# Attention block on one core: the last head pair's work spread evenly, 8 sums on TensorE, products on GpSimd, x loaded in 12 pieces

## What is computed

```python
xn = group_norm(x, 32 groups) * gn_w + gn_b
q, k, v = split(qkv_w @ xn + qkv_b)         # 8 heads of 64 channels
w = softmax(q^T k / sqrt(64))               # over the keys
a = v w^T                                   # 512 x T
out = xn + proj_w @ a + proj_b
```

## Time and profile before

| | before |
|---|---|
| median of 3 runs | 3740.59 us |
| lowest, highest | 3740.57, 3741.36 us |
| profiled execution, time | 3741.51 us |
| its span, first to last instruction | 3739.7 us |
| granted TensorE clock, mean | 0.998 |
| PE, PEld busy | 99%, 61% |
| DVE, ACT, POOL busy | 60%, 77%, 80% |
| instructions | 74752 |

### The profile page before, as it was taken

The page is one execution under the profiler, slowest core; times in us unless marked ns, Lnnn a source line. Parts: engine busy times, 40 slices in busy tenths (PEclk is TensorE's granted clock), DMA queues, the critical chain, the costliest instruction groups (busy, mean ns, idle before and its releaser), DMA issues.

```text
span 3739.7 us, 74752 instructions
## 1 busy us (share of the span) xinstructions
PE 3700.3 (99%) x30072; PEld 2267.9 (61%) x30072; DVE 2261.2 (60%) x2885; ACT 2875.0 (77%) x4091; POOL 2997.6 (80%) x1639
## 2 busy tenths in 40 slices
PE   8999999999999999999999999999999999999998
PEld 5565565656756565565675656556577565656556
DVE  6555657656565656665656565666655665565654
ACT  3777777787677777779767777777876777777885
POOL 1888888888388888888838888888875888888994
PEclk9999999999999999999999999999999999999999
DMA  2000012021400001201140000211222000000022
GB/s 81 21 17 26 23 32 73 17 61 37 148 19 23 17 23 39 67 23 55 52 133 25 18 23 17 60 50 28 68 65 101 23 23 19 23 17 20 20 88 89
DMA packets 131418, 165.03 MB, mean 44 GB/s; under 512 B 61696, under 2 KB 107776, under 8 KB 130176
## 3 DMA queue, kind: packets, MB, share of 16 engines
q1 hardware_dynamic: 131072, 160.26, 13.6%
HBM read 122.17 MB, written 38.04 MB: 43 GB/s over the span
## 4 chain that ended last, share of the span: by engine, by line
PE 93%; ACT 2%; POOL 2%; DVE 1%; issue 1%; DMA 0%; SPq 0%; ACTq 0%; POOLq 0%; DVEq 0%
PE oacc L648 29%; PE scores L627 23%; PE pool_bank L575 14%; PE aux_banks L597 12%; PE pool_bank L587 7%; PE scores L725 5%; POOL denom L1221 2%; PE pool_bank L614 1%; ACT probs L834 1%; ACT scores L847 1%; PE scores L575 1%; DVE maxima L953 1%; DVE stats L984 0%; PE scores L587 0%; DMA xn<-x 0%
## 5 line engine op out<-in xcount | busy, mean ns | idle before, releaser
L1221 POOL TENSOR_TENSOR denom<-denom,probs 128x768 f32<-128x768 f32 x1536 | 2821.9, 1837 | 422.0 <-ACT probs L834 230.6
L953 DVE TENSOR_REDUCE maxima<-aux_banks 128x2 f32<-128x512 f32 x1728 | 1655.9, 958 | 1305.8 <-PE aux_banks L597 1272.9
L834 ACT ACTIVATE probs<-scores 128x768 f32<-128x768 f32 x1728 | 1311.9, 812 | 679.7 <-PE scores L627 671.5
L847 ACT ACTIVATE scores<-seeds 128x768 f32<-128x768 f32 x1728 | 1342.6, 823 | 2.2 <-PE scores L635 1.5
L648 PE MATMUL oacc<-probs,vals 128*64 128x384 f32 x6912 | 1282.7, 492 | 0.0
L648 PEld LDWEIGHTS oacc<-probs,vals 128*64 128x64 f32 x6912 | 455.0, 136 | 522.7 <-issue 381.4
L597 PE MATMUL aux_banks<-k_hi,q_hi 64*128 64x512 f32 (+1 forms) x3456 | 681.3, 390 | 7.0 <-DVE maxima L953 6.4
L597 PEld LDWEIGHTS aux_banks<-k_hi,q_hi 64*128 64x128 f32 x3456 | 322.0, 183 | 534.8 <-issue 435.2
L627 PE MATMUL scores<-q_hi,k_hi 64*128 64x384 f32 x3456 | 597.4, 342 | 11.5 <-ACT scores L847 11.2
L627 PE MATMUL scores<-q_hi,k_lo 64*128 64x384 f32 x3456 | 586.5, 335 | 0.0
L627 PE MATMUL scores<-q_lo,k_hi 64*128 64x384 f32 x3456 | 586.0, 334 | 0.0
(11 more groups left out here) (93 smaller groups left out, 1534.0 us busy)
## 6 DMA issues: line engine op xcount, KB each, us to landing
seeds<-neg_rows SPq DMA_DIRECT2D x96, 384.0 KB, 3.5
xtile<-x SPq DMA_DIRECT2D x72, 384.0 KB, 3.2
att<-o_norm SPq DMA_DIRECT2D x96, 192.0 KB, 1.9
probs<-x SPq DMA_DIRECT2D x18, 768.0 KB, 4.5
out<-probs SPq DMA_DIRECT2D x18, 768.0 KB, 3.8
xtile<-att SPq DMA_DIRECT2D x12, 768.0 KB, 5.9
att_raw<-att SPq DMA_DIRECT2D x12, 768.0 KB, 6.8
xn<-x SPq DMA_DIRECT2D x7, 1152.0 KB, 12.7
```

The costliest lines, as they stand in the source:

```text
L834: a(prob(s).rearrange("p (h n) -> p h n", n=N), scores[:, s % 2, :, 0:N], ACT.Exp, scale=SCALE).then_inc(probs_ready, 1)
L847: a(scores[:, s % 2, :, 0:N], seeds[blk % 2][:, :].rearrange("p (e n) -> p e n", n=N), ACT.Copy).then_inc(seeded, 1)
L953: v.tensor_reduce(maxima[:, :, qt, kc], aux_banks[:, :, 0:UNIT_KEYS[kc % 2]], AX.X, ALU.max)\
L1221: gp.tensor_tensor(acc, acc, prob(s), ALU.add).then_inc(added, 1)
```

## The change

The last pair of a batch with a successor is planned by `SPREAD` like the inner ones, in the order own q, four k, one v, two k, two q, five v. The next batch's tiles are normalized from step 2, every 4 steps; each part waits for the own q chunks of its columns. `FINAL_OWN_Q` puts the quarters of the last batch's q chunks into the first 16 slots. The statistics of pair 2 stand at steps 30 to 52. The fourth piece (the product) is taken by GpSimd after the sum of the step before the put, for all blocks but the last of each batch and the last six of the last batch; the put is two steps later. In the last batch 8 of the last steps (3 in block 22, 5 in block 23, counted from 0) are not added by GpSimd: TensorE multiplies them with ones into the bank of the finish. In the last batch the odd chunks of `att` use `k_hi[0]` and `k_lo[0]`, and chunk 1 is split within the stream. x of the first batch comes in 12 transfers, and the weights are issued after the sixth has landed.

```diff
-    LAST_OWN_Q = ...
-    FINAL_OWN_Q = (((0, 0, 2), (1, 2, 4)), ((4, 0, 1), (6, 1, 2), (8, 2, 3), (10, 3, 4)),
-                   ((12, 0, 1), (14, 1, 2), (16, 2, 3), (18, 3, 4)), ((21, 0, 1), (23, 1, 2), (25, 2, 3), (27, 3, 4)))
-    LAST_RUNS = ((13, (1, 1, 2)), (16, (1, 1, 1, 1)),
-                 *((r + d, n) for r in (21, 30, 39) for d, n in ((0, (1, 1, 2)), (3, (1, 1, 2)), (6, (2, 2)))),
-                 *((r, (2, 2)) for r in (48, 50, 52)))
-    STATS_AT, STATS_EVERY = 28, 2
+    FINAL_OWN_Q = (((0, 0, 2), (1, 2, 4)), ((3, 0, 1), (4, 1, 2), (5, 2, 3), (6, 3, 4)),
+                   ((7, 0, 1), (8, 1, 2), (9, 2, 3), (10, 3, 4)), ((12, 0, 1), (13, 1, 2), (14, 2, 3), (15, 3, 4)))
+    STATS_AT, STATS_EVERY = 30, 2
-    NORM_AT, NORM_EVERY = 18, 2
+    NORM_AT, NORM_EVERY = 2, 4
...
+            if kind == LAST and more_batches:
+                items = own_q + next_k[0:4] + next_v[0:1] + next_k[4:] + next_q + next_v[1:]
+            elif kind == LAST:
+                items = []
+                for key, parts in zip(own_q, FINAL_OWN_Q):
+                    for s, a, b in parts:
+                        part(s0 + s, key, a, b)
+            else:
+                items = own_q + next_k + next_q + next_v
+            for n, key in enumerate(items):
+                for s, a, b in SPREAD[n % 3]:
+                    part(s0 + n // 3 * BLOCK_SLOTS + s, key, a, b)
...
-        att_hi = [att_hi0[:, :, :], four(k_hi[last_keys])]
-        att_lo = [att_lo0[:, :, :], four(k_lo[last_keys])]
+        def att_parts(tc, last):
+            keys = 1 - last_keys if last else last_keys
+            return (four(k_hi[keys]), four(k_lo[keys])) if tc % 2 else (att_hi0[:, :, :], att_lo0[:, :, :])
...
+        def summed_by_products(blk, kt, last):
+            return last and ((blk == BLOCKS - 2 and kt in (13, 15, 17)) or
+                             (blk == BLOCKS - 1 and kt in (9, 11, 13, 15, 17)))
+        def by_gpsimd(blk, last):
+            return blk < BLOCKS - (CH if last else 1)
         def put_at():
-            return {p * STEPS + fin_steps(j)[-1]: p * CH + j for p in range(PAIRS) for j in range(CH)
+            return {p * STEPS + fin_steps(j)[-1] + 2: p * CH + j for p in range(PAIRS) for j in range(CH)
...
-            for part in range(XPARTS):
+            for n in range(XITEMS):
+                i, part = n // XPARTS, n % XPARTS
                 cols_of = slice(part * XW, (part + 1) * XW)
-                sp.dma_start(xn[:, 0, cols_of], x[0, 0:128, cols_of]).then_inc(x00_in[part], 16)
-            for i in range(1, CT):
-                sp.dma_start(xn[:, i, :], x[0, i * 128:(i + 1) * 128, :]).then_inc(x0_in[i - 1], 16)
+                sp.dma_start(xn[:, i, cols_of], x[0, i * 128:(i + 1) * 128, cols_of]).then_inc(x0_in[n], 16)
+            sp.wait_ge(x0_in[XITEMS // 2 - 1], 16)
...
+            def sum_by_product(s, u, opens):
+                to = bank_for(u) if opens else bank(u)
+                for e in range(2):
+                    mm(to[head(e), 0:N], ones[:, :], prob(s)[:, e * N:(e + 1) * N], start=opens, stop=False)
...
+                if summed_by_products(s // KT, kt, last):
+                    sum_by_product(s, use(b, last, ("finish", p, t // KT)),
+                                   not any(summed_by_products(s // KT, k, last) for k in range(kt)))
...
-                            if NORM_STEPS[s] == 0:
-                                wait_full(act, use(b, last, ("q", PAIRS - 1, CH - 1)))
+                            if NORM_STEPS[s] and NORM_STEPS[s] % CT == 0:
+                                wait_full(act, use(b, last, ("q", PAIRS - 1, 2 * (NORM_STEPS[s] // CT) + 1)))
...
-                    if 0 <= n < CT:
-                        att_high(b, 0, slice(n, n + 1))
+                    if 0 <= n < (2 if last else 1) * CT:
+                        att_high(b, n // CT, last, slice(n % CT, n % CT + 1))
...
+                            if piece == PIECES - 1 and by_gpsimd(blk, last):
+                                continue
                             take_recip(b, blk, use(b, last, ("finish", blk // CH, blk % CH)), piece)
...
+                if summed_by_products(blk, kt, last):
+                    pool.wait_ge(added, PRIMED + ADDS * (BLOCKS * b + blk) + kt - 1)
+                    pool.sem_inc(added, 1)
+                    return
...
+            def normalize_block(n):
+                pool.wait_ge(recip_ready, PRIMED + n + 1)
+                pool.wait_ge(o_saved, PRIMED + n + 1)
+                pool.wait_ge(att_out, PRIMED + 16 * n)
+                gp.tensor_tensor(o_norm[:, :], o_raw[:, :], recip[:, :], ALU.mult).then_inc(o_normed, 1)
...
-                    add(s, b)
+                    add(s, b, last)
+                    blk = PUT_AT.get(s + 1)
+                    if blk is not None and by_gpsimd(blk, last):
+                        normalize_block(BLOCKS * b + blk)
```

More of the change, by code:

```diff
@@ L294, in attention_block_program @@
         x_in = [sem(f"x_in{i}") for i in range(XPARTS)]
-        x00_in = [sem(f"x00_in{i}") for i in range(XPARTS)]
-        x0_in = [sem(f"x0_in{i}") for i in range(1, CT)]
+        x0_in = [sem(f"x0_in{i}") for i in range(XITEMS)]
         consts_made = sem("consts_made")
@@ L385, in attention_block_program @@
         STATS_STEPS = {s: n for n, s in zip(range(XITEMS), (
-            s for s in range(STATS_S0 + STATS_AT, LAST_S0, STATS_EVERY) if s not in PUT_AT))}
+            s for s in range(STATS_S0 + STATS_AT, LAST_S0, STATS_EVERY)))}
         NORM_STEPS = {LAST_S0 + NORM_AT + NORM_EVERY * n: n for n in range(XITEMS)}
@@ L607, in group_var, with finish @@
                 filled(mm(bank_for(u)[:, 0:CT], groups[:, :], tmp, start=True, stop=True), u)
-            def finish(b, blk, u):
+            def sum_by_product(s, u, opens):
+                to = bank_for(u) if opens else bank(u)
+                for e in range(2):
+                    mm(to[head(e), 0:N], ones[:, :], prob(s)[:, e * N:(e + 1) * N], start=opens, stop=False)
+            def finish(b, blk, u, last_batch):
                 pe.wait_ge(added, PRIMED + ADDS * (BLOCKS * b + blk + 1))
-                to = bank_for(u)
+                opens = not any(summed_by_products(blk, kt, last_batch) for kt in range(KT))
+                to = bank_for(u) if opens else bank(u)
                 for e in range(2):
                     last = mm(to[head(e), 0:N], ones[:, :], denom[:, blk % 2, e * N:(e + 1) * N],
-                              start=True, stop=True)
+                              start=opens, stop=True)
                 filled(last, u)
@@ L683, in behind @@
                 elif kind == "finish":
-                    finish(b, p * CH + i, u)
+                    finish(b, p * CH + i, u, last)
                 elif kind == "groupmean":
@@ L711, in projection @@
                 for tc in range(CH):
-                    i = tc % 2
                     if tc == 2:
-                        finish(b, BLOCKS - 1, use(b, last, TAIL))
+                        finish(b, BLOCKS - 1, use(b, last, TAIL), last)
                         if not last:
@@ L718, in projection @@
                     pe.wait_ge(att_lo_ready, CT * (CH * b + tc + 1))
+                    hi, lo = att_parts(tc, last)
                     for ot in range(CT):
@@ L722, in projection @@
                             pe.wait_ge(proj_saved, PRIMED + PJ * b + n - 3)
-                        for w, a in ((wproj_hi, att_hi[i]), (wproj_lo, att_hi[i]), (wproj_hi, att_lo[i])):
+                        for w, a in ((wproj_hi, hi), (wproj_lo, hi), (wproj_hi, lo)):
                             for k in range(CT):
                                 ins = mm(scores[:, n // 2 % 2, n % 2, 0:N], w[:, k, ot * 128:(ot + 1) * 128],
-                                         a[:, k, :], start=(w is wproj_hi and a is att_hi[i] and k == 0),
-                                         stop=(a is att_lo[i] and k == CT - 1))
+                                         a[:, k, :], start=(w is wproj_hi and a is hi and k == 0),
+                                         stop=(a is lo and k == CT - 1))
                         ins.then_inc(proj_full, 1)
@@ L812, in save_o, with att_high @@
                 a(o_raw[:, :], oacc[:, 0:N], ACT.Copy).then_inc(o_saved, 1)
-            def att_high(b, tc, rows=slice(0, CT)):
+            def att_high(b, tc, last, rows=slice(0, CT)):
                 i = tc % 2
@@ L897, in projection @@
                     if n % CT == CT - 1 and n // CT + 2 < CH:
-                        att_high(b, n // CT + 2)
+                        att_high(b, n // CT + 2, last)
                     if n == PJ - 3 and not last:
@@ L973, in take_stats @@
                     tile = xn[:, i, part * XW:(part + 1) * XW]
-                    if i == 0:
-                        dve.wait_ge(x00_in[part], 16)
-                    elif part == 0:
-                        dve.wait_ge(x0_in[i - 1], 16)
+                    dve.wait_ge(x0_in[n], 16)
                 else:
```

(9 more changed lines are left out.)

31 lines of the change are left out of this document (10 added, 21 removed).

## The result

Five runs of each on one chip: the kernel before 3740.59 us (3739.59 to 3741.36), the changed kernel 3721.66 us (3719.26 to 3721.87). That is 18.9 us or 0.5% less, a ratio of 0.9946 with a 95% interval of 0.9936 to 0.9957. The forecast was 3727.3, the range 3720 to 3737. The profiled execution of the changed kernel is the fastest of the five, 3719.26 us around a span of 3717.6, so between the two profiled executions there are 22.1 us of span to explain; why this one stands 2.4 us under the others comes up with the clock.

The account below looks back on a forecast made before the run. TensorE, busy 99% of the span, was taken as the bound. Terms -9.9 + 0 + 0 + 0 - 2.4 - 1.0 = -13.3 us gave 3728.2 us profiled, 3727.3 at the median; range 3720 to 3737.

Parts of the forecast that it names:

- Last pairs: Last pair of three batches with a successor: spread chunks, thinned normalizations gain 3.3 of 3.92 us each, -9.9 us.
- Rival A: Last pairs: ScalarE stays late, normalizations also spoil 3.7 us slots; 0 to 1.3 us per batch gained; 3736; chance 0.12.
- Pair 2: Statistics two steps earlier change nothing, +-0.5 us; taking products off VectorE gains nothing in inner pairs.
- no inner slot is late by them: Inner pairs: VectorE's products delay no slot, as theirs is a long one, so removing them gains nothing.
- Products on GpSimd: 87 of 96 multiplications move to GpSimd at 1.0 us each, hidden under TensorE's 35.87 us block: 0 us.
- rival B: Every block of inner pairs: GpSimd becomes the bound if product, gap and waits exceed 2.22 us; 3751; chance 0.08.
- Last pair of the last batch: Last batch's last pair: -5.1 for the wait gone, +3.6, +0.8 and 0 to 1.5 against: about 0, ends -3, +2.
- Rival C: Last batch's last pair: sums on TensorE cost 5.9, not 2.8 us, clock costs in full; +4.5, 3732; chance 0.06.
- Tail: Last projection: the 2.44 us wait for ScalarE's high part of the second chunk goes, -2.4 us.
- Start: First loads: twelve transfers bring statistics sooner, but coefficients wait for constants until 22.0 us; -1.0 us, ends 0 and 2.4.
- rival D: Whole kernel better than summed: the whole 3.92 three times, start 2.4, stream -3; about 3720; chance 0.06.

Follow-up runs that it names:

- e2: Changed kernel with only the normalizations put back to every second step from step 18, the even chunk order kept; 3726.95 us, one run.
- e4: Changed kernel with the products of all blocks given back to VectorE; 3726.43 us, ratio 0.9962.
- e6: Changed kernel with chunk 1's split after the stream again and x in six transfers with the weights directly behind; 3722.80 us, one run.
- e8: The changed kernel measured a second time, unchanged; 3720.30 us (3720.26 to 3722.65).
- e7: Changed kernel with two more sums on TensorE, key tiles 15 and 17 of block 21 in the last batch; 3717.66 us, ratio 0.9941.
- e11: The kernel of e7 measured again, beside the changed kernel on the same chip; 3717.55 us, ratio 0.9932.

## Why the prediction was right and where not

The direction and the range held, the range with 1.7 us to its lower end; the sum was 13.3 us where the profiles show 22.1 and the medians 18.9. Term by term:

- Last pairs, -9.9 forecast, -11.9 measured. The mechanism held. I kept 0.6 us a batch back for a ScalarE that runs late in slots with a normalization and a high part; e2 shows that such slots, with a chunk in each, are as long as others even in a row. Some 0.2 us a batch come from VectorE's products instead. Rival A fell with it.
- Pair 2, 0 forecast for the statistics and for the products, -2.1 measured over three batches. The statistics give 0.3 us a batch: I had compared whole pairs and not looked at the slot of 4.06 us in which VectorE's maxima were late by 0.28 us behind a statistic. The rest came with the products, but by no product's own slot: "no inner slot is late by them" held for the slots with a product in this pair, 4.33 us before and 4.35 after in slot 23. What the sum lacked is that VectorE's coefficient steps last until GpSimd's running sum ends, and that a product among the sums changes when that is.
- Products on GpSimd, 0 for inner pairs: right, pairs 0 and 1 differ by 0.12 us in all. 1009 ns against the 1.0 us taken, and rival B fell. The Trainium skill, GPSIMD Engine Reference, "Engine selection", would have kept them on VectorE. There they take 549 ns at best in e4, which agrees with its factor of two, but 1812 ns in the mean, nearly twice GpSimd's time.
- Last pair of the last batch, 0 forecast, -3.6 measured, just beyond the end of -3. The place of the waits was right: one at block 21, none at block 22. Up to the first finish the stream grew by 0.3 us and not 0.8: 3609.39 - 3470.07 = 139.32 against 3624.86 - 3485.84 = 139.02. PE came there 1.9 us sooner and not 3, so it waited 2.57 us for a forecast of 4; the clock behind this wait cost 0 or 1.35 us, within my 0 to 1.5. From this finish to the projection it went from 57.17 to 53.27 us, -3.9, where I had -5.1 + 2.8 + 0.8 = -1.5. Two terms were mis-sized. The kernel before has these rows, the first scores of the second slot behind block 22's finish and of the last slot:

```profile
3665.02 0.44 PE L627 MATMUL scores<-q_hi,k_hi 64*128 64x384 f32 x2
...
3677.85 0.44 PE L627 MATMUL scores<-q_hi,k_hi 64*128 64x384 f32 x2 [0.25 <-ACT scores L847]
```

  The old wait with its slow clock was worth 5.9 us and not 5.1: its slot and the next took 12.67 us, now 6.74. The sums and the high parts together cost 2.0 us and not 3.6: 3662.66 - 3643.73 = 18.93 against 3682.03 - 3665.02 = 17.01 is 1.9 with five of the sums, and 0.1 in the slots of the other three. The price is not even: the last slot, with two sums, takes 3662.66 - 3657.37 = 5.29 us where 3682.03 - 3677.85 = 4.18 stood, and the slot before it 0.16 more with one. The split alone costs nothing that shows (e6). Rival C fell.
- Tail, -2.4 forecast, -2.7 measured: right in size, wrong in cause. The wait was put down to ScalarE's high part; it was VectorE's low part, and the sums on TensorE alone take it away as well.
- Start, -1.0 forecast, -1.55 measured: the order of causes was as worked out, with the constants ending last; only their landing was 0.6 us sooner than the 22.0 that I worked out. This size is in part luck, as other profiles of the same start stand 0.7 us earlier to 4.6 us later.

The outcome lies nearest to rival D, which had 0.06: all of pair 3, and 3 us in the last stream (its terms add up to 3721.0, not 3720). Each term but products had been taken on its cautious side, and they all erred the same way; a range wide enough on that side, and not the sum, is what held.

## What to carry to other kernels

Where a busy engine sets the pace, compare like stretches (the same slots of equal pairs) with each other: the pair with the uneven order was 3.92 us longer and gave back all of it. Spreading and feeding belong together: either edit alone gave about half. When a wait is moved, look at where it lands and give it the same remedy there: two more sums took away the last 2.57 us, for 1.0 us of their own. Compare the same slot when slots are compared: a slot of 4.35 us beside one of 3.76 says nothing. And before an edit is costed against a wait, look for the row that ends about 0.1 us before its end, on every engine; the releaser that a profile names need not be it.

## What the runs showed of the hardware

- VectorE's instructions with two tiles of SBUF as operands ran on to the end of the GpSimd sum beside which they began. In the kernel before this holds for all 84 products that began during a running sum: they took 548 to 2221 ns, and each ended 0.41 to 0.52 us behind the end of that sum. The coefficient steps of slots 43 and 44, of 128x4, took up to 1.68 us and ended 0.02 or 0.03 us behind it. Low parts of keys and queries, of which one operand lies in PSUM, took 606 to 618 ns during the sums as well. Four low parts of `att`, 128x384 each, took 8.27 or 7.42 us beside sums and 2.20 with none, and the sums beside them up to 1.97 us in place of 1.83. A product of 128x384 took VectorE 1812 ns in the mean (e4) and GpSimd 1009.
- The granted clock of TensorE isn't settled by the program: after equal waits of 2.57 us it fell to 0.50 (1.2 GHz) in e8 and stayed at 1.00 (2.4 GHz) in the first profile. A wait of 0.97 us before the first slot was followed by 0.50 from 77.7 to 81.1 us in e7, whose first slot took 4.57 us, and by no fall in e11, the same kernel, where it took 3.11. At the start too: in e4 it stood at 0.50 until 32 us, and the first k matmuls took nearly twice as long, with the first slot at 82.41 us in place of 77.78 (1.7 us of this are the late constant). The rows are those of e4 and of the changed kernel:

```profile
26.82 5.39 PE L579 MATMUL scores<-xn,wk 128*64 128x384 f32 x16 [1.73 <-ACT xn L820]
```

```profile
25.10 2.80 PE L579 MATMUL scores<-xn,wk 128*64 128x384 f32 x16 [0.27 <-issue]
```

So a single run can't tell edits of this kernel apart by less than some 4 us (the 15 runs of the changed kernel go from 3718.88 to 3722.65); the lengths of undisturbed stages, which repeat to about 0.2 us, can.
